# First chunk of a masked FFN layer: counts of pieces three and four turned by DMA, and the selects' equality marks in a free PSUM bank

## What is computed

```
xn    = layernorm(x)
s     = xn @ (block-masked W).T + bias
inter = xn @ c1.T @ c2.T                      # rank 16, 1792 wide
idx   = argmax of each block of 32 of inter   # 56 blocks
h     = relu(w1[idx] . xn)                    # one kept row for each block
g     = h @ w2t[idx]
x     = x + s * silu(g)
```

## Time and profile before

| | us |
|---|---|
| median of 3 runs | 633.07 |
| lowest, highest | 631.99, 633.42 |
| the profiled execution | 631.34 |
| its span, first to last instruction | 629.6 |

### The profile page before, as it was taken

One profiled execution on the slowest core, in us unless ns is written; L12 is line 12 of the kernel. 1 busy time (PEld: TensorE's weight loads), 2 busy tenths in 40 slices (PEclk: granted clock), 3 DMA queues, 4 the chain that ended last, 5 costly groups with the idle time before them and its releaser, 6 DMA issues.

```text
span 629.6 us, 8344 instructions
## 1 busy us (share of the span) xinstructions
PE 615.4 (98%) x2852; PEld 498.4 (79%) x2852; DVE 454.0 (72%) x718; ACT 217.7 (35%) x388; POOL 246.5 (39%) x194
## 2 busy tenths in 40 slices
PE   7999999999999999999999999999999999999997
PEld 4678787878888878888878887787878878887886
DVE  7988768888767788768777786686468448835844
ACT  6443333412223312224213243643245135414610
POOL 3455655650000650000741454477316532642543
PEclk9999999999999999999999999999999999999999
DMA  9951000033420034410142622272137034300701
GB/s 265 400 218 35 1 33 2 25 102 100 135 51 9 26 100 117 116 50 8 31 142 75 221 84 75 84 185 69 38 116 184 18 117 111 91 33 35 203 18 50
DMA packets 51951, 59.41 MB, mean 94 GB/s; under 512 B 29136, under 2 KB 29520, under 8 KB 50896
## 3 DMA queue, kind: packets, MB, share of 16 engines
q1 hardware_dynamic: 51776, 58.98, 31.0%
q10 hardware_dynamic: 144, 0.03, 0.0%
HBM read 44.96 MB, written 8.53 MB: 85 GB/s over the span
## 4 chain that ended last, share of the span: by engine, by line
PE 82%; DVE 11%; DMA 3%; issue 2%; ACT 1%; POOL 0%; SPq 0%; DVEq 0%; ACTq 0%
PE bank L453 76%; DVE counts L1060 3%; DVE seg_top L1046 2%; DVE eq L1048 2%; PE bank L1342 1%; PE bank L357 1%; PE bank L1320 1%; DMA first<-counts 1%; DMA prod<-expert_weights 1%; PE bank L1504 1%; DVE h L1081 1%; DVE h_lo L1096 1%; DVE x_tile L397 1%; PE bank L1361 1%; DVE prod L1200 0%
## 5 line engine op out<-in xcount | busy, mean ns | idle before, releaser
L429 POOL TENSOR_TENSOR g_tile<-g_tile,s_tile 128x512 f32<-128x512 f32 x31 | 45.5, 1467 | 158.8 <-DVE g_tile L1114 93.1
L860 ACT ACTIVATE h_hi<-h 128x512 fp32r<-128x512 f32 x56 | 35.4, 633 | 160.6 <-DVE h L1081 158.3
L453 PE MATMUL bank<-w_hi_t,h_hi 128*128 128x512 f32 x224 | 89.6, 400 | 0.3
L453 PE MATMUL bank<-w_lo_t,h_hi 128*128 128x512 f32 x224 | 87.6, 391 | 0.0
L453 PE MATMUL bank<-xT_hi,w_hi_t 128*128 128x512 f32 x224 | 87.3, 390 | 0.0
L453 PE MATMUL bank<-w_hi_t,h_lo 128*128 128x512 f32 x224 | 87.3, 390 | 0.0
L453 PE MATMUL bank<-xT_lo,w_hi_t 128*128 128x512 f32 x224 | 87.2, 389 | 0.0
L453 PE MATMUL bank<-xT_hi,w_lo_t 128*128 128x512 f32 x224 | 87.2, 389 | 0.0
L1060 DVE TENSOR_TENSOR_SCAN counts<-restart,eq 128x512 bf16<-128x512 bf16 (+1 forms) x56 | 75.0, 1340 | 2.0
L1046 DVE TENSOR_REDUCE seg_top<-bank 128x16 f32<-128x512 f32 (+1 forms) x64 | 39.5, 618 | 42.0 <-PE bank L1342 42.0
L773 POOL TENSOR_TENSOR prod_lo<-prod,prod_hi 128x512 fp32r<-128x512 f32 x32 | 49.1, 1565 | 27.9 <-ACT prod_hi L923 27.9
(11 more groups left out here) (201 smaller groups left out, 1243.1 us busy)
## 6 DMA issues: line engine op xcount, KB each, us to landing
prod<-expert_weights SPq DMA_DIRECT2D x32, 256.0 KB, 5.6
w_raw<-in_w SPq DMA_DIRECT2D x28, 256.0 KB, 10.2
x_res<-in_x SPq DMA_DIRECT2D x4, 1024.0 KB, 8.4
mid_state<-g_tile SPq DMA_DIRECT2D x16, 256.0 KB, 2.1
x_tile<-mid_state SPq DMA_DIRECT2D x4, 1024.0 KB, 5.4
x_res<-mid_state SPq DMA_DIRECT2D x4, 1024.0 KB, 8.5
out<-g_tile SPq DMA_DIRECT2D x15, 256.0 KB, 2.0
row<-in_x SPq DMA_DIRECT2D x12, 256.0 KB, 2.6
```

What stands on the lines that cost most here:

```text
L429: nc.gpsimd.tensor_tensor(g_tile[:, tt, :], g_tile[:, tt, :], s_tile[:, tt, :], ALU.mult).then_inc(s_free, 1)
L453: last = nc.tensor.matmul(dst, a, b, start=(start and n == 0), stop=(stop and n == len(mms) - 1))
L860: nc.scalar.activation(h_hi[:, it % 2, :], h[:], ACT.Copy).then_inc(h_hi_done, 1)
```

## The change

Four edits (lines stand 2 to 10 numbers higher in the changed file than before).

1. In chunk 0, PE turns only pieces 0 and 1 (BY_PE = 2). The six groups of four transposes for blocks 8 to 13 are gone from PE.
2. Pieces 2 and 3 of chunk 0 are counted into `counts` and turned by eight DMA transposes from SP, put between and behind `moments_out` and `moments_in`. The ones for piece 3 wait until PE has read the piece in the second half of `first` (`first_tr` 8).
3. DVE's h of blocks 8 to 13 in chunk 0 reads its mask from `first` in SBUF, where it read bank 7, and waits for the DMAs.
4. The eq of the selects goes to `marks`, which is bank 7 as float32, wherever that bank is free: piece 0 of chunk 0 and all pieces of chunks 1 to 3. In chunk 0, pieces 1 to 3 stay in `eq`.

```
+        marks = banks[7]
+        BY_PE = 2
...
             for tt in range(TT):
-                sp.sem_inc(ld_first[tt], PIECES * 16)
+                sp.sem_inc(ld_first[tt], BY_PE * 16)
             next_row(0, 0)
             next_rows(0, x_turned[1])
             for tt in range(1, TT):
                 next_row(0, tt)
+            turn(0, 2, 0)
             moments_out(0)
+            for tt in range(1, TT):
+                turn(0, 2, tt)
             moments_in(0)
+            sp.wait_ge(first_tr, 4 * BY_PE)
+            for tt in range(TT):
+                turn(0, 3, tt)
             rows_out(0, mid_rows[0])
...
-                nc.vector.tensor_tensor(eq[:, 0:PW[p]].rearrange("p (s n) -> p s n", n=SEG), got,
+                place = eq if opens(c) and p else marks
+                nc.vector.tensor_tensor(place[:, 0:PW[p]].rearrange("p (s n) -> p s n", n=SEG), got,
...
-                if not opens(c):
+                if not opens(c) or p > BY_PE:
                     dve.wait_ge(ld_first[tt], (c * PIECES + p) * 16)
...
-                kept = first_counts[p % 2] if opens(c) else counts
-                nc.vector.tensor_tensor_scan(kept[:, tt, 0:PW[p]], restart[:, 0:PW[p]], eq[:, 0:PW[p]], 0.0,
+                kept = first_counts[p] if opens(c) and p < BY_PE else counts
+                place = eq if opens(c) and p else marks
+                nc.vector.tensor_tensor_scan(kept[:, tt, 0:PW[p]], restart[:, 0:PW[p]], place[:, 0:PW[p]], 0.0,
...
-                    if opens(c):
+                    if opens(c) and it < 4 * BY_PE:
                         dve.wait_ge(first_tr, it + 1)
                         which = first_bank
...
-                    if first:
+                    if first and it <= 4 * BY_PE:
                         first_transpose(it - 1)
```

## The result

| | before | after |
|---|---|---|
| median | 633.25 us (4 runs) | 628.30 us (4 runs) |
| lowest, highest | 631.99, 634.15 | 627.77, 628.79 |
| the profiled execution | 631.34 | 628.77 |
| its span | 629.6 | 627.0 |

The ratio is 0.9927, with a 95% interval of 0.9913 to 0.9942: 0.73% faster, 4.95 us. The forecast was 628.3.

The account below looks back on a forecast made before the run. PE bounds the kernel, busy 615.4 of 629.6 us, standing still where DVE's selects come late. Terms -5.0 - 1.2 + 1.8 - 0.4 = -4.8 us gave 626.5 for the profiled execution, 628.3 for the median; range 624.6 to 631.7.

Parts of the forecast that it names:

- Heads of chunks 1 to 3: First selects of the bodies: scans with eq in PSUM take 1.22 us, PE's waits go; 5.0 us gained (1.76 + 2 x 1.64).
- Head of chunk 0: Shorter scans bring the first transposes 1.65 us earlier; the first h_lo then costs PE 0.45; 1.2 us gained.
- Price of eq in PSUM: DVE writing eq to PSUM and scanning from it costs 0; upper bound 0.69 us more per eq.
- The six groups of transposes: Chunk 0, blocks 8 to 13: PE is rid of 1.9 us, gained only if DVE kept up, which it does not.
- The tail of chunk 0: Last blocks: h with its mask in SBUF takes turns with POOL's adds; 1.8 us lost (1.9 gained to 2.6 lost).
- The DMA turns: Chunk 0, pieces 2 and 3: 1.2 us to issue, 2.3 to land, hidden between scan and h; counted 0.
- End of layer one: Chunk 3: POOL's next instruction starts earlier, so an h PE waits for is shorter; 0.4 us gained (0 to 0.6).
- From the profiled execution to the median: -4.8 us takes the profiled 631.3 to 626.5; that execution lay 1.7 under the median 633.07, so the median becomes 628.3.
- (a): Rival, chunk 0's last blocks: PE keeps up to 1.9 us of the removed transposes; 624.6 to 626.5 us; chance 0.22.
- (c): Rival, select chain of the heads: PSUM forms are dear; no gain at 0.3 us more each, 636.5 at 0.4; chance 0.05.
- (d): Rival: a scan with one PSUM input still takes turns with POOL; heads unchanged, tail costs 1.8; 634.9 us; chance 0.04.
- (b): Rival: PSUM eq or scan costs 0.1 to 0.25 more, or chunks 1 to 3's first h_lo delays PE; 630 to 632.6; chance 0.16.

Follow-up runs that it names:

- the marks alone: Kernel before with only eq of the free selects moved to bank 7; PE still turns all counts of chunk 0: 625.35 us, ratio 0.9878.
- the other input in PSUM: Kernel before with eq still in SBUF, but restart copied to bank 7 as float32 and scanned from there in chunks 1 to 3: 627.30 us, ratio 0.9928.
- eq's type alone: Kernel before with eq as float32 instead of bfloat16, still in SBUF: 632.84 us, ratio 1.0003.
- marks and early adds but no DMA turns: Kernel before with eq in bank 7 and POOL's bias scaling and s_tile adds moved earlier; PE keeps chunk 0's transposes: 625.96 us, ratio 0.9909.
- the turns alone: Changed kernel with eq back in SBUF everywhere, leaving edits 1 to 3: 635.67 us, ratio 1.0046.
- the early adds: Changed kernel with POOL's bias scaling and four s_tile adds of chunk 0 moved before its row statistics: 624.18 us (0.9864), again 625.31 us (0.9892).
- the second profile: Kernel before, unchanged, run and profiled once more: median 632.68 us, ratio 0.9998; profiled execution 632.96 us, for 631.34 in the first.
- the c2 part later: Kernel of the early adds with DVE's second c2 rest part in chunk 0's head moved behind the second select: 625.06 us, ratio 0.9878.

## Why the prediction was right, step by step

**Heads of chunks 1 to 3: right.** Counted 1.76, 1.64, 1.64; the trace shows 1.74, 1.63, 1.65, the marks alone 1.77, 1.63, 1.64. Every scan is at 1.22, the first selects do not wait, and the first `h_lo`, named as next to be late, is not: PE goes on to it with no bracket. The mechanism (one DVE input in PSUM ends the turns with POOL) was shown from both sides, by the other input in PSUM and by eq's type alone. The Trainium skill (SBUF — State Buffer, "SBUF: two separate sides") states the same as an exclusive lock, taken by DVE with two SBUF inputs; these runs agree, with 1.225 us at worst against 2.199.

**Head of chunk 0: right in kind, 0.25 too much.** Counted 1.2, seen 0.95. The first transposes came 1.65 us nearer to the second select (10.48 for 12.13), exactly as counted. What was mis-sized is the loss behind: `h_lo` shows 1.64 where it took 0.68, and PE gives back 0.70, not 0.45. Part of it is how a wait is read: the bracket says 0.50, but the first down product starts 0.90 after the transposes (39.28 to 40.18) where it started 0.21 after them before, so 0.69 is lost. A start-to-start distance is the safer measure.

**Price of eq in PSUM: right.** 8 ns for each eq, nothing for the scan. The scan has a median of 1220 ns with a PSUM input and of 1224 without. The Trainium skill (VectorE: DVE Perf Modes, "The TRN2 errata") gives PSUM sources 62 cycles more; these rows show nothing of it.

**The six groups of transposes: right, a little high.** Counted 1.9 and not gained; 0.56 of it shows until it = 12. When DVE keeps up, the kernel with the groups gone is 1.58 ahead over the stretch (-1.83 for -0.25 with marks and early adds but no DMA turns).

**The tail of chunk 0: right, with some luck in the parts.** Counted 1.8 lost, seen 1.86 from it = 9 to the next chunk (-0.56 and +2.42), and 1.91 in the turns alone. The predicted order (h, shift, h_lo, scale, h) is in the rows, the last four at about 1.77. Not all of it is as walked through: the first h was to wait for the first add and waited beside the scaling of the bias instead, and the last h was to go free behind the fourth add. It took a turn too, because POOL's adds began later than counted: at 102.04 for 100.17, that is 1.26 us later with the program's start taken off, where up to 0.8 was allowed. These misses hardly move the sum of the tail. The select that opens the stretch came 0.56 earlier, not 0.65 to 0.95, and the h of blocks 8 and 9 do meet POOL (1.71 us each), which moves `turned_shift` of it = 9 into a turn too. The remedy, POOL's adds elsewhere, shows that these turns and not the DMAs are the cause.

**The DMA turns: right at 0.** A turn takes a median of 2.4 us, and no h of chunk 0 waits for one. SP's rows of the changed kernel show three of them between the moments' way out and way in; the row at 79.62 is the last of the three seen by itself:

```profile
71.72 9.51 SPq L513 DMA_TRANSPOSE first<-counts  x3
79.62 1.62 SPq L513 DMA_TRANSPOSE first<-counts  x1
81.29 1.20 SPq L551 DMA_DIRECT2D bias_b<-moments  x1
```

The moments' way in is issued at 81.29, where it was 79.69 before: 1.0 us later with the program's start taken off, for 0.5 counted. No instruction behind waits for them.

**End of layer one: right.** The h beside POOL is shorter, as counted:

```profile
381.09 1.27 DVE L1091 SCALAR_TENSOR_TENSOR h<-first,h 128x512 f32<-128x512 bf16 x1
```

It was 1.71. PE reaches the transposes of the next rows 0.43 us nearer (387.76 for 390.82, at a distance of -2.63 before), for 0.4 counted. PE waited 0.49 us there before and does not now, and the gain lasts until layer two's last chunk, where PE is at -3.17. It is not this gain that is given back at the end: in both traces of the early adds the same 0.43 arises and lasts to the last instruction (-7.97 and -6.57 there, -7.95 and -6.52 behind layer one).

**From the profiled execution to the median.** The sum was -4.8. Up to layer two's last chunk the trace has -4.73 without the program's start: 0.25 is missing at head 0 and 0.06 at the tail, and 0.1 each came on top at layer one's end (0.49 over that stretch, for 0.4) and in layer two's first chunk. The late weights of the last chunk, which the prediction has no term for, leave -4.16. The median nevertheless moved by 4.95. The prediction compared with a profiled execution 1.7 us under its median; the second profile shows that 1.4 us of such a distance can arise in layer two, where nothing was edited. So the sum is right stretch by stretch, and that 628.3 met 628.30 to the tenth is luck: what layer two does from one execution to the next is larger than that.

**The rivals.** (a), the transposes' time shows, fell for this kernel and came true in the one with early adds. (c) and (d) fell with the scan rows. Of (b) neither condition came true (eq costs 8 ns more, and the first `h_lo` of chunks 1 to 3 is in time); head 0 gave less for another reason, its own first `h_lo`.

## What to carry to other kernels

When a DVE instruction with two SBUF inputs shows twice its usual duration beside POOL, put either input into an idle PSUM bank; price the reverse move, from PSUM to SBUF, by what POOL does at that place. Cost each part of a change by itself: here one part alone brought 7.7 us by the medians (6.1 by the traces), the others took about 2 of it by the traces, and they paid only after POOL's work was moved away. Compare traces by the distance between starts of the same instruction, stretch by stretch, and profile the unchanged kernel twice before explaining a microsecond.

## What the runs showed of the hardware that was not expected

- Executions of one program differ at fixed places. PE's second select of chunk 0 starts between 23.83 us (the early adds) and 25.97 (the c2 part later), and in two executions of one kernel at 23.83 and 25.15; behind it, the distance of two profiles of the kernel before changes by no more than 0.05 us for 358 us. The next place is layer two, where the wait for the expert weights' DMA is 2.56 us in one execution of a kernel and 1.47 in another.
- A wait of 0.50 us in a bracket cost PE 0.69 from start to start. The row behind a wait also shows 0.50 where the others show 0.39, and the next starts 0.33 later (40.18 to 40.51), not 0.23.
- One kernel (the early adds) gave a ratio of 0.9864 in one comparison and 0.9892 in another, on another chip, each with an interval of 0.0015 to either side.
